# Attention by batch: transfers of one batch, a first group of one tile, an alternating order in layer 1, and the rows of the maxima issued from POOL

## The reference

```python
qh = q.reshape(b * h, d // h, m)
kh = k.reshape(b * h, d // h, -1)
vh = v.reshape(b * h, c // h, -1)
scale = 1.0 / jnp.sqrt(jnp.asarray(d // h, dtype=q.dtype))
qk = jnp.einsum('bdm,bdn->bmn', qh, kh) * scale
```

## Time and profile before

| | us |
|---|---|
| median of 3 runs | 1435.39 |
| lowest, highest | 1432.31, 1446.13 |
| the profiled execution | 1445.65 |
| its span | 1443.9 |

### The profile page before, as it was taken

One profiled execution on the slowest core, in us unless ns is written; L12 is line 12 of the kernel. 1 busy time (PEld: TensorE's weight loads), 2 busy tenths in 40 slices (PEclk: granted clock), 3 DMA queues, 4 the chain that ended last, 5 costly groups with the idle time before them and its releaser, 6 DMA issues. The chain is left out here.

```text
span 1443.9 us, 19040 instructions
## 1 busy us (share of the span) xinstructions
PE 1122.5 (78%) x6658; PEld 793.4 (55%) x6658; DVE 668.4 (46%) x1365; ACT 624.0 (43%) x978; POOL 524.3 (36%) x579
## 2 busy tenths in 40 slices
PE   0589813474867998579948999999976758999997
PEld 0245501332436886235527888888843446888886
DVE  4657667520116334747745333333366953333333
ACT  3245738333654433245634334334354433333332
POOL 2025400010113664002224665666611034665663
PEclk9989956666887999578968999999988958999999
DMA  6545130136411431534112335323210003334331
GB/s 195 140 120 163 51 116 1 37 96 152 114 45 60 128 102 51 132 94 123 49 49 80 114 102 172 115 102 115 78 26 1 2 23 117 104 108 118 104 106 65
DMA packets 62354, 132.34 MB, mean 92 GB/s; under 512 B 8859, under 2 KB 32219, under 8 KB 58774
## 3 DMA queue, kind: packets, MB, share of 16 engines
q1 hardware_dynamic: 62294, 131.56, 30.8%
HBM read 115.49 MB, written 15.45 MB: 91 GB/s over the span
## 5 line engine op out<-in xcount | busy, mean ns | idle before, releaser
L1224 POOL TENSOR_TENSOR f_hid<-f_gated,f_coef 128x512 f32<-128x512 f32 x152 | 223.9, 1473 | 173.8 <-DVE f_gated L1255 161.8
L1255 DVE TENSOR_TENSOR f_gated<-f_act_g,f_p_u 128x512 f32<-128x512 f32 x152 | 104.4, 687 | 274.2 <-PE f_p_u L1087 270.5
L706 ACT ACTIVATE a_probs<-a_p_sc 128x1024 f32<-128x1024 f32 x192 | 185.6, 1017 | 42.3 <-PE a_p_sc L636 38.1
L780 DVE TENSOR_REDUCE a_maxes<-a_p_max 128x2 f32<-128x512 f32 x256 | 159.4, 680 | 70.1 <-PE a_p_max L604 69.7
L1164 ACT ACTIVATE f_hid_hi<-f_hid 128x512 fp32r<-128x512 f32 x152 | 96.1, 632 | 208.7 <-POOL f_hid L1224 208.6
L1259 DVE TENSOR_TENSOR f_hid_lo<-f_hid,f_hid_hi 128x512 fp32r<-128x512 f32 x152 | 105.5, 694 | 150.9 <-ACT f_hid_hi L1164 150.5
L636 PE MATMUL a_p_sc<-a_q,a_k 75*128 75x256 bf16 (+1 forms) x768 | 126.6, 298 | 53.9 <-ACT a_probs L706 36.5
L1159 ACT ACTIVATE f_act_g<-f_p_g 128x512 f32<-128x512 f32 x152 | 90.8, 597 | 170.3 <-PE f_p_g L1087 170.3
L604 PE MATMUL a_p_max<-a_k,a_q 72*128 72x256 bf16 x512 | 99.1, 319 | 67.6 <-DMA a_k<-k_plain 30.1
L636 PEld LDWEIGHTS a_p_sc<-a_q,a_k 75*128 75x128 bf16 (+1 forms) x768 | 73.0, 105 | 104.7 <-issue 53.1
L655 PE MATMUL a_p_out<-a_probs,all_v 128*32 128x256 f32 x1536 | 123.1, 460 | 4.8 <-ACT a_probs L706 4.8
(11 more groups left out here) (272 smaller groups left out, 1727.4 us busy)
## 6 DMA issues: line engine op xcount, KB each, us to landing
f_w<-in_w SPq DMA_DIRECT2D x76, 384.0 KB, 3.5
f_coef<-coef SPq DMA_DIRECT2D x51, 512.0 KB, 3.8
a_q<-q_parts SPq DMA_DIRECT2D x24, 576.0 KB
a_k<-k_plain SPq DMA_DIRECT2D x48, 192.0 KB
outs<-a_out SPq DMA_DIRECT2D x48, 128.0 KB, 2.2
a_whole<-outs SPq DMA_DIRECT2D x48, 128.0 KB, 2.6
a_k<-k_unit SPq DMA_DIRECT2D x24, 192.0 KB
all_v<-in_v SPq DMA_DIRECT2D x4, 1024.0 KB, 6.6
```

Source lines behind the costliest of these rows:

```text
L706: nc.scalar.activation(probs[b % 2][:, 2 * pair:2 * pair + 2, :, :].rearrange("p h t d -> p h (t d)"), p_sc[pair % 2][:], ACT.Exp, scale=s ...
L780: nc.vector.tensor_reduce(maxes[b % 3][:, :, h], p_max[:, n % 3, :].rearrange("p (t d) -> p t d", t=NK), axis=AX.X, op=ALU.max, negate=Tru ...
L1224: nc.gpsimd.tensor_tensor(hid[c][:], gated[c][:], coef[slot(t, 2)][:, c * 512:(c + 1) * 512], ALU.mult).then_inc(hid_done, 1)
L1255: nc.vector.tensor_tensor(gated[c][:], act_g[c][:], p_u[c][:], ALU.mult).then_inc(gated_done, 1)
```

## The change

All of it lies in the three attentions.

- **By batch.** q and k lie in SBUF in 8 slots of one batch instead of 4 of a pair; `load_q(b)` and (layers 0 and 2) `load_k(b)` move one batch. `load_k` of layer 1 stays with pairs. SP issues the loads of batch b+4 in iteration b, ahead of `store_out(b-1)`; `load_whole(b-2)` comes first.
- **First tile alone.** `CUTS` becomes tiles 0, 1, 2-3, 4-5, 6-7 and `LN_CUTS` tile 0 and the rest. The layer norm of tiles 2 to 7 is applied by ACT (`apply_by_act`, with a shift from DVE). POOL splits the later groups alone (`all_on_pool`, four instructions a group). Six stores a group stay.
- **UnitKeys in a0.** Load at b = 0; squares and sums by POOL (15 instructions in iterations 2 to 4); clamp and inverse on DVE among the maxima (n = 60 and n = 64), the root on ACT after `exps(5, 3)`; the splits in iterations 6 to 13 instead of 3 to 10.
- **HeadNorm in a1.** Tile 0 alone first; the seven others by one ACT square and seven matmuls; their inverses are spread in steps 0 to 3.
- **The order.** Layer 1 follows `"0w1x2yz3"`, with `copy_out` between `exps(b, 2)` and `exps(b, 3)`; step 0 of the others follows `FIRST_ORDER`, and AHEAD is 16. `weigh` waits for the exponentials of its half only.
- **Maxima rows.** `load_neg(b+1)` is issued by POOL, at the head of POOL's iteration b, instead of SP.
- **The end.** Four buffers of `whole`, two of `inv`; tiles 6 and 7 are multiplied and added by DVE (`add_late`). The inverses among the maxima are cut into four.

```diff
-CUTS = ((0, 2), (2, 4), (4, 8))
-ROW = HEADS * 2 * D
+CUTS = ((0, 1), (1, 2), (2, 4), (4, 6), (6, 8))
+ROW = HEADS * D
...
+FIRST_ORDER = "0mm1mmtmm2mm3mmt"
 STEP_ORDER = "mm0mm1wxmmyz2mm3t"
-AHEAD = 18
+PLAIN_ORDER = "0w1x2yz3"
+AHEAD = 16
+SLOTS = 8
...
                 for b in range(B):
-                    if b >= 3:
-                        load_whole(b - 3)
                     if b >= 2:
-                        store_out(b - 2)
-                    if with_max and b + 2 < B:
-                        load_neg(b + 2)
...
+                        load_whole(b - 2)
+                    if layer == 1:
+                        if b == 0:
+                            store_q(1, 0)
+                            store_q(1, 1)
+                            load_q(2)
+                            load_unit_pair(2)
+                            load_q(3)
+                        if b in (1, 2, 3):
+                            store_q(b + 1, 0)
+                            store_q(b + 1, 1)
...
+                    elif b + 4 < B:
+                        load_k(b + 4)
+                        load_q(b + 4)
+                    if b >= 1:
+                        store_out(b - 1)
+                    if with_max and b in (1, 3):
+                        if layer == 0:
+                            store_k(b // 2 + 3)
+                        store_q(b // 2 + 3, 0)
+                        store_q(b // 2 + 3, 1)
...
                     odd, t = quarter // 2, quarter % 2
+                    if t == 0:
+                        pe.wait_ge(exp_done, PAIRS * b + 2 * (odd + 1))
                     if quarter == 0:
-                        pe.wait_ge(exp_done, PAIRS * (b + 1))
...
+                else:
+                    pool.wait_ge(norm.xn_by_act, 2)
+                    parts.all_on_pool(pool, one, 2)
+                    split_max(0)
+                    if layer == 0:
+                        split_key(3)
+                    load_neg(0)
+                    split_max(1)
+                    load_neg(1)
+                    pool.wait_ge(norm.xn_by_act, NI - 2)
+                    parts.all_on_pool(pool, one, 3)
+                    split_max(2)
+                    if layer == 0:
+                        key_parts.all_on_pool(pool, one, 4)
+                    split_max(3)
+                    load_neg(2)
+                    parts.all_on_pool(pool, one, 4)
+                    for b in range(2, B):
+                        if b + 1 < B:
+                            load_neg(b + 1)
+                        if b >= 6 and b % 2 == 0 and b // 2 - 3 < 4:
+                            add_tile(b // 2 - 3)
+                        if b + 2 < B:
+                            split_max(b + 2)
```

More of the change, by code:

```diff
@@ L180, with __init__ @@
 class Parts:
-    def __init__(self, st, tag, src, dram, cuts=CUTS, part=None):
-        self.nc, self.src, self.dram, self.cuts = st.nc, src, dram, cuts
+    def __init__(self, st, tag, src, late, part=None):
+        self.nc, self.src, self.late = st.nc, src, late
         self.part = st.sb(f"{tag}_part", [P, 3, NI, D], BF16) if part is None else part
[L186 to L190, removed]
@@ L204, in pool_high @@
[L204 to L213, removed]
+        t = slice(*CUTS[g])
@@ L220, in take_mid @@
+        tt(self.src[:, t, :], self.src[:, t, :], self.part[:, 0, t, :],
+           ALU.subtract).then_inc(self.pick(self.rest_ready, g)[0], 1)
     def take_mid(self, eng, tt, g):
[L221 to L232, removed]
@@ L517, in load_ones @@
                     src = ones[:]
-                    src = bass.AP(src.tensor, src.offset, [list(src.ap[0]), [0, RING * HEADS], [1, 2 * D]])
-                    sp.dma_start(k[MAX_AT:MAX_AT + 3, :, :, :, :], src).then_inc(ones_loaded, 16)
-                def store_group(g):
-                    if layer == 0:
-                        for part in range(3):
-                            key_parts.store(sp, part, g)
-                    for part in range(3):
-                        parts.store(sp, part, g)
@@ L568, in _ @@
                 for b in range(B):
-                    if b >= 3:
-                        load_whole(b - 3)
                     if b >= 2:
-                        store_out(b - 2)
-                    if with_max and b + 2 < B:
-                        load_neg(b + 2)
-                    if b == 0 and layer == 0:
-                        for part in range(3):
-                            key_parts.store(sp, part, 2)
-                        load_v(1)
-                    if b == 1:
-                        for part in range(3):
-                            parts.store(sp, part, 2)
-                        wait_group(2)
@@ L799, in _ @@
                     unit.invert(dve, 1)
[L800 to L802 removed]
+                    for i in range(1, NI):
+                        unit.scale(dve, i)
                 else:
@@ L882, in _ @@
                 if layer == 0:
-                    for g in range(len(CUTS)):
-                        key_parts.take_high(pool, tt, g)
-                        key_parts.take_mid(pool, tt, g)
+                    for g in range(3):
+                        split_key(g)
                 if layer == 1:
-                    pool.wait_ge(unit.out_ready, 2)
-                    parts.pool_high(one, 1)
-                    parts.pool_mid(pool, one, 1)
-                    pool.wait_ge(unit.out_ready, 4)
@@ L891, in _ @@
-                    parts.pool_high(one, 2)
-                    parts.pool_mid(pool, one, 2)
-                if with_max:
-                    for b in range(2):
-                        split_max(b)
-                for b in range(B):
-                    if with_max and b + 2 < B:
-                        split_max(b + 2)
-                    if b >= 5 and b % 2 == 1:
-                        add_tile(b // 2 - 2)
-                    if layer == 0 and 3 <= b < 3 + CH:
-                        if b == 3:
-                            wait_keys(pool)
-                        for what in range(5):
-                            unit_keys.split(pool, one, what, b - 3)
```

648 lines of the change are left out of this document (399 added, 249 removed).

## The result

The changed kernel takes 1402.3 us (median of 4 runs, 1398.6 to 1404.7) against 1437.0 (median of 4, one more than when the prediction was made) for the kernel before: 0.973 of it, with a 95% interval from 0.968 to 0.978. It is faster, as forecast, but by 35 us and not by 110, and it lies above the range's upper end of 1366. The span of its profiled execution is 1402.3 us against 1443.9, a gain of 41.6.

A forecast was written before the change was run, and what follows sets the result against it. SP's order and the long preparation, not an engine, were taken to bound the three attentions. Gains of 34.6 (a0), 45 (a1) and 30.4 us (a2) sum to 110, taking the median 1435.39 to 1325; range 1300 to 1366.

The forecast's parts named there:

- POOL's issue: Maxima rows issued by POOL: taken to cost POOL 0.83 us each, as on SP, for an a0 iteration of 6.4 us.
- (2): Rival: POOL becomes the bound of a0 and a2, with 3 us for each `load_neg`; 1349 us, chance 0.12.
- (3): Rival: slower than before, POOL's transfer late for every step of a0 and a2, about 7 us in all; chance 0.02.
- the round of 5.1 us: a1 until batch 12: SP's issues plus waiting 2 to 4 us for the last store, 5.1 us a step on average.
- its own sign of being wrong: a1: the prediction is wrong if SP's round comes out above 6 us.
- Rival (1): Layer 1 stays on a half-cold PE, twelve steps of 6.69 us, 80 instead of 61; 1344 us, chance 0.15.
- a0, the start: Start of a0: q of batch 1 lands at 25.2, first scores at 33, 23.7 us earlier than 56.70.
- undisturbed steps of 6.55 us: a0 steps 2 to 13 and twelve steps of a2: 12 x 6.55 = 78.6 us.
- one pause of 5 us: a0 after `exps(5, 3)`: unit keys' root and DVE's inverse hold PE's maxima, 5 us with the cold PE behind it.
- are covered by loads that run four batches ahead: a0: later parts' stores, nine issues at b = 1 and 3, 6 us of SP's queue, would stop no step.
- a2, the start: Start of a2: first scores at 595 instead of 605.6; steps 0 and 1 take 19.5 us.
- one rival with part of another: Range's upper end, 1366 us: Rival (1) with (2) in part; sums of two rivals were said to lie beyond.

The follow-up runs named there:

- k1: Changed kernel with SP loading back, in iteration b, the result of batch b-3 instead of b-2; 1374.1 us, 0.952 of the kernel before.
- k7: k1 with layer 0's values in 16 loads of 256 KB, four behind batch 3's loads, and POOL's starting list reordered; 1363.8 us, 0.939 of the kernel before.
- k4: Changed kernel with ACT copying the unit keys' lengths instead of taking their root, dropping two table loads; 1401.9 us, 0.972 of the kernel before.
- k5: k1 with DVE's inverses of results and unit keys later among the maxima, POOL's unit-key splits one batch later; 1361.2 us, 0.940 of the kernel before.
- k10: k9 with an extra unused DVE inverse of growing size in three steps of layer 2; steps 7.3, 10.5, 13.0 us against 7.0, 7.1, 7.0.
- k9: k1 with k5's and k7's edits, layer 1's early q loads, POOL's last parts and unit-key work one batch later; 1353.9 us, 0.939 of the kernel before.
- k8: k1 with layer 1's old order of scores and value products and the copy ahead of the third exponential; 1380.3 us, 0.950 of the kernel before.

## Why the prediction was wrong

**What held.** The direction, and that the gain lies in starts and waits: a1's first scores came 19.0 us into the stage (20.3 predicted) and batch 4's at 52.0 (51). The 19.43 us wait of a copy is gone. POOL's issue takes 0.60 us (0.83 taken), so rivals (2) and (3) fall. A pause for DVE's inverse stood behind step 5, and POOL's split held the turn of step 0 for 2.69 us (3).

**a1, the round of 5.1 us.** This is the term that failed most. The step in the text is "behind a quarter to a half of that I take 2 to 4 us". In front stood a quarter (288 KB of q) and three quarters (0.86 of 1.15 MB) in turn, since k of layer 1 stays with pairs. The landing took 3.7 to 3.9 us behind the first and 5.6 to 6.5 behind the second, the round 6.9, above the 6 that the prediction named as its own sign of being wrong. From the scores of batch 4 (307.47) to the last copy (387.11) it is 79.6 us instead of 62: 17.6 of the stage's 19.8. I had seen that SP waits for the store issued last and had made it the bound of eight steps, but only 0.6 us above the 4.5 that ACT and PE need, instead of asking what takes it away. k1 did: 115.9 us, below even the 120.5 forecast, because a step there takes ACT's 4.4 us and not 5.05. Rival (1), a half-cold PE, named the right size (steps of 6.69, measured 7.0) for a cause that was second: the low clock followed from the waits, since the same order ran at 0.98 in k1, where the changed kernel had 0.81.

**a0, the start.** q of batch 1 landed at 30.6 instead of 25.2, and the first scores came at 38.45 instead of 33: 5.5 us. I had let `load_v(0)` cost its issue and a little more, but batch 1 also waits for a store behind it and then for a load; without it in front, k7's wait was 0.82 us.

**a0 and a2, the loops.** I multiplied undisturbed steps of 6.55 us by twelve and added one pause of 5 us. Steps without a wait did take 6.5, but not all were: from the scores of batch 2 (60.80) to the last copy (171.27) a0 took 110.5 us instead of 94.8, a2 99.0 instead of 89.8. Two things were missing. The sentence that the nine later stores "are covered by loads that run four batches ahead" was wrong, because SP had spent that lead on the store's landing in each round; k1 and k4 show two causes of the step of 16.7 us, and k5 the step without either, 7.8. And waits were priced too low: the root's pause at 5 us, where with the inverse behind it it made a step of 14.0 out of 6.5 (k1), and others at their own length, where two measured ones cost twice that (k10). The two last steps of a0 lost 1.5 us each on the low clock, with 32 products at 3.4 to 3.5 us.

**a2, the start.** First scores 25.3 us into the stage instead of 21.4, and steps 0 and 1 24.9 us instead of 19.5, with waits of 2.75, 2.69 and 1.25 us on a slow clock. k7 took back 3.8 us of the stage.

**The range.** Its upper end was one rival with part of another. The largest terms fell short together: a1's round by 17.6 us, the loops of a0 and a2 by 15.7 and 9.2, the starts of a0 and a2 by 5.5 and 3.9, the first two steps of a2 by 5.4. That they went the same way I put down to what they share, SP's queue and PE's clock; for a1 and the late loads of a0 k1 shows it, for the rest it is argued. I had left sums of two rivals out as unlikely; with a shared cause they come together.

## What to carry to other kernels

When a queue waits for a transfer that it issued itself just before, count its round as issues plus landing behind all that was put ahead of it, and compare that with the step: if it comes within a quarter, treat it as the bound. Here moving one load back by one iteration was worth 24 us in a stage of 140.

Price a wait of PE at about twice its length where the step is full, and a loop of good steps as what is left once every late arrival is placed. Causes that end in the same step hide each other, so an experiment that removes one of them can show little (k4), and two executions of the same code show how far a step varies by itself.

## What was not expected of the hardware

- A 128 KB store took 1.7 us to land in k1's a1 from batch 12 on, where no loads of q and k stand in front of it any more. In the changed kernel's a1 it took 3.7 to 3.9 behind 288 KB of q, and 5.6 to 6.5 behind 0.86 MB (288 KB of q and three times 192 KB of k).
- A transfer issued by POOL cost it 0.60 to 0.73 us. Its 12 KB landed after 2.8 us in the median of the changed kernel's a0, but after 5.7 in its slowest case there, and in k9 the scores waited until 5.8 us after the issue with the DMA engines 75% busy. The Trainium skill (DMA: Bandwidth & Descriptors, Queues, rings and completion order) says that each DMA engine takes turns between the queues that have work for it; no run here shows the turns themselves, only that POOL's rows, though in a queue of their own, could be that late among SP's transfers.
- The low clock came with pauses as short as 0.77 and 0.23 us in a step, repeated (k8), and after two waits of together 1.7 us (k10).
